# Weight stream of a graph and transformer kernel: one transfer for three weight blocks, on two semaphores, into the same six slots

## The chip, the cores and the metric

One Trainium2 chip, one core. The metric is the device time of one execution in microseconds (us); lower is better. Engines: TensorE (PE, its weight loads PEld), VectorE (DVE), ScalarE (ACT), GpSimd (POOL) and SyncE (SP), which here only issues the DMA transfers of the weight stream.

## The reference, cut to what matters

Four rounds over 512 nodes with 768 features. Each round adds a graph layer, an attention mixer and a feed-forward part to `x`. All work is matrix products in fp32 with 768x768 tiles of weights; the graph layers read 16,384 edges. The change touches only how weights reach the chip, so two of the feed-forward parts matter most. In round 1 (`ffn1` in the kernel) and in round 3 (`ffn3`), most weights meet few columns:

```
# round 1: 506 patch rows use fc1, fc2; 6 class rows use five small "atom" networks
patch_out = gelu(patch_tokens @ fc1_w.T + fc1_b) @ fc2_w.T + fc2_b
hid_all = gelu(einsum('bnd,ahd->bnah', cls_tokens, atom_in_w) + atom_in_b)
...
# round 3: 8 experts, each takes at most 64 of the 512 rows
expert_inputs = einsum('td,tec->ecd', xf, dispatch)
h = gelu(einsum('ecd,edm->ecm', expert_inputs, w1) + b1)
expert_outputs = gelu(einsum('ecm,emd->ecd', h, w2) + b2)
out = einsum('ecd,tec->td', expert_outputs, combine)
```

## The kernel before, in words

**The stream.** All weights but one lie in one DRAM tensor, `stream`, as blocks of 128 x 768 fp32 (384 KB), in the order of use. Six blocks are a turn; the kernel has 93 turns, 558 blocks (`TURNS`). On the chip `raw` has six slots, `raw[:, g, j]` with g = 0, 1 and j = 0, 1, 2; block b of each turn goes to slot g = b // 3, j = b % 3. SP (L317 to L338) issues one transfer per block, `load(n, b)`, on six semaphores `raw_in[b]`, one to a slot. It issues the first six at once. Each later one waits until that slot's previous block is free.

**Split stages.** In all parts but `ffn1` and `ffn3` each raw block is split by POOL in `split` (L354 to L363): `w_hi` is the block rounded to a shorter float, `w_lo` the rest. POOL waits for the load (`raw_in[b]`) and for TensorE to give back the split slot (`w_used`), then counts up `w_split`; with that the raw slot is free, and SP waits on `w_split` for the next load. TensorE makes three matmuls per tile from the split pairs (`mm3`, L409 to L416).

**Whole stages.** In `ffn1` (4 turns) and `ffn3` (6 turns), named in `WHOLE`, TensorE reads the raw slots itself. `whole_block(turn, b)` (L400) waits for `raw_in[b]`, and after a block `whole_block_used()` (L403, the matmul at L404) runs a tiny matmul that counts up `raw_used`, which SP waits for. `ffn1` multiplies at L971 (12 blocks; all but two meet 8 columns), then at L984 and L992 (12 blocks). `ffn3` has 16 blocks of 64 columns at L1056 and two that no one multiplies, and after ScalarE's last gelu (L1493) 18 blocks at L1069, in the last turn with 8 matmuls a block instead of 12. The tail behind them (L1077 and on) loads nothing.

**Stretches.** `stretches` lists runs of turns of one kind (split, whole, split, whole). At the start of each run SP waits on the semaphore of the run before, since those blocks hold the slots.

The matrix `L0_gnn_W1` is also loaded by ScalarE's own queue into a ring of eight slots (`w_ring`, `scr`), which the change does not touch.

Of the kernel before, what the change touches and what calls it, by code (L numbers as in the profile page):

```python
# [33 lines left out]
KC = D // P  # L34
# [149 lines left out]
def build(nc, t, out, only=None, LOOP_EVENTS={}):  # L184
# [3 lines left out]
    for p in parts:  # L188
        whole, n = p in WHOLE, sum(s[1] for s in stretches)
# [5 lines left out]
    with ctx:  # L195
        def sb(name, shape, dt=F32, where=ctx):
            return where.enter_context(nc.sbuf_tensor(name, shape, dt))

        def sem(name):
            return ctx.enter_context(nc.semaphore(name))  # L200

        raw = sb("raw", [P, 2, 3, KC, P])
# [91 lines left out]
        loaded, edges_in, rows_in, orf_in, sel_in = (sem(n) for n in ("loaded", "edges_in", "rows_in", "orf_in", "sel_in"))  # L295
        setup_done = sem("setup_done")
        pool_done = sem("pool_done")
        raw_in = [sem(f"raw_in{b}") for b in range(6)]
        w_high, w_split, w_used = sem("w_high"), sem("w_split"), sem("w_used")
        raw_used = sem("raw_used")  # L300
        tile_for = {"act": sem("tile_for_act"), "dve": sem("tile_for_dve")}
# [15 lines left out]

        @block.sync
        def _(sp):
            def load(n, b):  # L320
                sp.dma_start(raw[:, b // 3, b % 3], t["stream"][bass.ds(n * 6 + b, 1)].rearrange(
                    "o p (k c) -> (o p) k c", k=KC)).then_inc(raw_in[b], 16)

            for b in range(6):
                load(0, b)
            freed = raw_used if stretches[0][2] else w_split
            for n, (first, count, whole, before) in enumerate(stretches):
                if n > 0:

                    for b in range(6):  # L330
                        sp.wait_ge(freed, freed_turns * 6 + (b - 5))
                        load(first, b)
                freed, freed_turns = raw_used if whole else w_split, before + count
                with sp.Fori(1, count) as i:
                    for b in range(6):

                        sp.wait_ge(freed, i * 6 + (before * 6 + b - 5))
                        load(i + first, b)  # L338

        @block.gpsimd
        def _(pool):
            pool.memset(ident[:, :], 0.0).then_inc(pool_done, 1)
            pool.wait_ge(pool_done, 1)
            pool.affine_select(out=ident[:, :], in_=ident[:, :], compare_op=ALU.not_equal, fill=1.0, base=0,
                               pattern=[[-1, P]], channel_multiplier=1).then_inc(setup_done, 1)
            pool.iota(iota[:, :], pattern=[[1, N]], base=0, channel_multiplier=0).then_inc(setup_done, 1)
            pool.memset(ones[:, :], 1.0).then_inc(setup_done, 1)
            pool.memset(ones_r[:, :].bitcast(F32), 1.0).then_inc(setup_done, 1)
            pool.memset(ones_b[:, :], 1.0).then_inc(setup_done, 1)  # L350
            pool.memset(nv[:, :, :], 0.0).then_inc(setup_done, 1)
            pool.memset(hot[:, :, :, :], 0.0).then_inc(setup_done, 1)

            def split(turn, n, b):  # L354

                pool.wait_ge(raw_in[b], turn * 16 + 16)
                if n > 0:
                    pool.wait_ge(w_used, n * 6 + (b - 5))
                pool.tensor_scalar(w_hi[:, b // 3, b % 3], raw[:, b // 3, b % 3], 1.0, 1.0, ALU.mult, ALU.mult)\  # L359
                    .then_inc(w_high, 1)  # L360
                pool.wait_ge(w_high, n * 6 + (b + 1))
                pool.tensor_tensor(w_lo[:, b // 3, b % 3], raw[:, b // 3, b % 3], w_hi[:, b // 3, b % 3], ALU.subtract)\  # L362
                    .then_inc(w_split, 1)  # L363

            pool.wait_ge(setup_done, n_setup)
            for first, count, whole, before in stretches:
                if not whole:
                    for i in range(count):
                        for b in range(6):
                            split(first + i, before + i, b)  # L370
# [3 lines left out]
        def _(pe):  # L374
# [23 lines left out]
                          skip_group_check=True).then_inc(w_used, n)  # L398

            def whole_block(turn, b):  # L400
                pe.wait_ge(raw_in[b], turn * 16 + 16)

            def whole_block_used():  # L403
                pe.matmul(ps[0:2, 7, 0:2], ones_b[:, :], ones_b[:, :], start=True, stop=True,  # L404
# [2 lines left out]
            def first_turn(p):  # L407
                return sum(TURNS[q] for q in parts[:parts.index(p)])
# [544 lines left out]
            if part("ffn1"):  # L953
# [7 lines left out]
                turn = first_turn("ffn1")  # L961
                for n in range(2):
                    for f in range(KC):
                        q = 6 * n + f
                        c = slice(0, N if q < 2 else 8)
                        whole_block(turn + n, f)
                        use(f)
                        for k in range(KC):
                            if q == 0:
                                pe.wait_ge(dve_to_pe, normed[k])  # L970
                            mm = pe.matmul(ps[:, f, c], raw[:, f // 3, f % 3, k], acc[:, k, c], start=k == 0,  # L971
                                           stop=k == KC - 1, skip_group_check=True)
                        done(mm, f, "act")
                        whole_block_used()
                pe.wait_ge(dve_to_pe, S.due(dve_to_pe))
                for n in range(2):
                    for f in range(KC):
                        whole_block(turn + 2 + n, f)
                        if n == 0:
                            use(f)  # L980
                            for k in range(2):
                                if f == 0:
                                    pe.wait_ge(act_to_pe, S.due(act_to_pe))
                                mm = pe.matmul(ps[:, f], raw[:, f // 3, f % 3, k], scr[:, k], start=k == 0, stop=k == 1,  # L984
                                               skip_group_check=True)
                            done(mm, f, "dve")
                            if f == 0:
                                use(6)

                        o = ps[:, 6, (6 * n + f) * 8:(6 * n + f) * 8 + 8]  # L990
                        for k in range(2, KC) if n == 0 else range(KC):
                            mm = pe.matmul(o, raw[:, f // 3, f % 3, k], scr[:, 3, (6 * n + k) * 8 - 16:(6 * n + k) * 8 - 8],  # L992
                                           start=k == (2 if n == 0 else 0), stop=k == KC - 1, skip_group_check=True)
                        whole_block_used()
# [30 lines left out]
            if part("ffn3"):  # L1025
# [19 lines left out]
                turn = first_turn("ffn3")  # L1045
                for n in range(3):
                    for f in range(KC):
                        q = 6 * n + f
                        whole_block(turn + n, f)
                        if q < 16:  # L1050
                            use(f)
                            c = slice(64 * (q // 2), 64 * (q // 2) + 64)
                            for k in range(KC):
                                if q == 0:
                                    pe.wait_ge(act_to_pe, S.due(act_to_pe))
                                mm = pe.matmul(ps[:, f, c], raw[:, f // 3, f % 3, k], acc[:, k, c], start=k == 0,  # L1056
                                               stop=k == KC - 1, skip_group_check=True)
                            done(mm, f, "act")
                        whole_block_used()
                for n in range(3):  # L1060
                    if n == 0:
                        pe.wait_ge(act_to_pe, S.due(act_to_pe))
                    for f in range(KC):
                        whole_block(turn + 3 + n, f)
                        use(f)
                        for e in range(3 * n, min(3 * n + 3, 8)):
                            for h in range(2):
                                k, q = 2 * (e - 3 * n) + h, 2 * e + h
# [1410 lines left out]
```

## Time and profile before

| | before |
|---|---|
| median of 3 runs (lowest to highest) | 3600.44 us (3599.62 to 3601.2) |
| the profiled execution's own time | 3605.52 us |
| its span | 3603.7 us |
| TensorE busy | 3221.0 us (89%) |
| VectorE busy | 1747.3 us (48%) |
| GpSimd busy | 1420.6 us (39%) |
| ScalarE busy | 753.7 us (21%) |
| mean granted TensorE clock | 0.923 of 2.4 GHz |
| bytes moved by DMA | 256.76 MB, mean 71 GB/s |
| weight transfers | 558 of 384 KB |

### The profile page before, as it was taken

The page shows a single profiled execution, that of the slowest core. Times are in us where ns is not written, and L with a number is a line of the kernel's source. Part 1 is how long each engine was busy: PE and PEld are TensorE (multiplying, and loading weights), DVE is VectorE, ACT ScalarE, POOL GpSimd, SP SyncE. Part 2 cuts the span into 40 slices and gives each one's busy share as a digit, 9 for nine tenths or more (in the row PEclk, how much of TensorE's full clock was granted, in tenths as well). Part 3 has the DMA queues.
Part 4 walks back from the last instruction along what each step waited for, and adds up shares of the span by engine and source line. Part 5 has one row for each costly group of instructions (what it writes and reads, how often), then busy time and mean ns, then how long its engine had stood idle before and what let it go on. Part 6 is the DMA issues. An engine that isn't in the chain of part 4 may idle for free.

```text
span 3603.7 us, 41581 instructions
## 1 busy us (share of the span) xinstructions
PE 3221.0 (89%) x14631; PEld 2527.2 (70%) x14631; DVE 1747.3 (48%) x2950; ACT 753.7 (21%) x1318; POOL 1420.6 (39%) x1008
## 2 busy tenths in 40 slices
PE   8878988799999996998966698989999998979978
PEld 2356667678888884676755467768888886768868
DVE  6633359756554536336676514724333346651131
ACT  0133320033332312102123212211101112221122
POOL 2011137635344440563520013436676764426500
PEclk9989999799999996999978779989999999989977
DMA  2011136412122220232210041213232332213313
GB/s 75 5 35 31 31 107 219 152 49 75 57 61 73 74 69 13 68 92 62 74 40 9 1 132 49 66 55 94 90 96 89 103 93 73 64 41 92 92 36 115
DMA packets 91012, 256.76 MB, mean 71 GB/s; under 512 B 10287, under 2 KB 10927, under 8 KB 90612
## 3 DMA queue, kind: packets, MB, share of 16 engines
q1 hardware_dynamic: 80352, 219.45, 20.1%
q10 hardware_dynamic: 10548, 35.83, 2.8%
q8 instruction: 69, 1.13, 0.1%
q14 instruction: 43, 0.35, 0.0%
HBM read 253.67 MB, written 1.57 MB: 71 GB/s over the span
## 4 chain that ended last, share of the span: by engine, by line
PE 82%; DVE 10%; issue 4%; ACT 2%; POOL 1%; DMA 0%; DVEq 0%; ACTq 0%; POOLq 0%
PE ps L411 21%; PE ps L415 20%; PE ps L416 20%; PE ps L831 3%; PE ps L507 2%; PE ps L513 2%; PE ps L1069 1%; PE ps L743 1%; PE ps L940 1%; DVE aux L1695 1%; PE ps L736 1%; PE ps L722 1%; PE ps L971 1%; PE ps L726 1%; POOL w_lo L362 1%
## 5 line engine op out<-in xcount | busy, mean ns | idle before, releaser
L359 POOL TENSOR_SCALAR w_hi<-raw 128x768 fp32r<-128x768 f32 x498 | 454.4, 913 | 1949.1 <-PE ps L411 1579.0
L362 POOL TENSOR_TENSOR w_lo<-raw,w_hi 128x768 fp32r<-128x768 f32 x498 | 973.0, 1954 | 41.6
L411 PE MATMUL ps<-H_hi,w_hi 128*128 128x512 f32 x804 | 321.6, 400 | 36.0 <-issue 28.8
L411 PE MATMUL ps<-B_hi,w_hi 128*128 128x512 f32 x720 | 292.2, 406 | 32.7 <-DVE B_lo L1536 22.3
L415 PE MATMUL ps<-H_lo,w_hi 128*128 128x512 f32 x804 | 319.1, 397 | 0.0
L416 PE MATMUL ps<-H_hi,w_lo 128*128 128x512 f32 x804 | 318.5, 396 | 0.0
L411 PE MATMUL ps<-A_hi,w_hi 128*128 128x512 f32 x780 | 308.2, 395 | 0.0
L415 PE MATMUL ps<-A_lo,w_hi 128*128 128x512 f32 x780 | 304.9, 391 | 0.0
L416 PE MATMUL ps<-A_hi,w_lo 128*128 128x512 f32 x780 | 303.9, 390 | 0.0
L415 PE MATMUL ps<-B_lo,w_hi 128*128 128x512 f32 x720 | 284.5, 395 | 0.0
L416 PE MATMUL ps<-B_hi,w_lo 128*128 128x512 f32 x720 | 284.0, 394 | 0.0
L411 PEld LDWEIGHTS ps<-H_hi,w_hi 128*128 128x128 f32 x804 | 154.9, 193 | 76.4 <-issue 38.7
L1790 DVE TENSOR_TENSOR x<-ps,x 128x512 f32<-128x512 f32 x102 | 70.5, 691 | 273.6 <-PE ps L416 270.1
L411 PEld LDWEIGHTS ps<-B_hi,w_hi 128*128 128x128 f32 x720 | 137.5, 191 | 71.4 <-issue 42.2
L411 PEld LDWEIGHTS ps<-A_hi,w_hi 128*128 128x128 f32 x780 | 146.9, 188 | 44.6 <-issue 12.9
L416 PEld LDWEIGHTS ps<-H_hi,w_lo 128*128 128x128 f32 x804 | 154.8, 192 | 33.3
L415 PEld LDWEIGHTS ps<-H_lo,w_hi 128*128 128x128 f32 x804 | 154.8, 193 | 32.4 <-issue 0.2
L416 PEld LDWEIGHTS ps<-A_hi,w_lo 128*128 128x128 f32 x780 | 147.0, 188 | 31.2
L415 PEld LDWEIGHTS ps<-A_lo,w_hi 128*128 128x128 f32 x780 | 147.0, 189 | 29.2
L415 PEld LDWEIGHTS ps<-B_lo,w_hi 128*128 128x128 f32 x720 | 137.7, 191 | 30.2 <-issue 3.1
L416 PEld LDWEIGHTS ps<-B_hi,w_lo 128*128 128x128 f32 x720 | 137.5, 191 | 29.7
L411 PE MATMUL ps<-w_hi,H_hi 128*128 128x384 f32 x432 | 147.5, 342 | 3.0 <-ACT aux L1190 3.0
(423 smaller groups left out, 6206.5 us busy)
## 6 DMA issues: line engine op xcount, KB each, us to landing
raw<-stream_dram SPq DMA_DIRECT2D x558, 384.0 KB, 3.0
w_ring<-w_dram ACTq DMA_DIRECT2D x24, 384.0 KB, 3.6
scr<-w_dram ACTq DMA_DIRECT2D x24, 384.0 KB, 3.9
u_rows<-rows_dram ACTq DMA_DIRECT2D x8, 768.0 KB, 6.1
rows<-rows_dram ACTq DMA_DIRECT2D x7, 768.0 KB, 4.0
x<-x_dram ACTq DMA_DIRECT2D x1, 1536.0 KB, 8.9
out_dram<-x ACTq DMA_DIRECT2D x1, 1536.0 KB, 5.1
orf<-orf_dram ACTq DMA_DIRECT2D x3, 384.0 KB, 4.0
```

Of the source, the lines that this page charges most:

```text
L359: pool.tensor_scalar(w_hi[:, b // 3, b % 3], raw[:, b // 3, b % 3], 1.0, 1.0, ALU.mult, ALU.mult)\
L362: pool.tensor_tensor(w_lo[:, b // 3, b % 3], raw[:, b // 3, b % 3], w_hi[:, b // 3, b % 3], ALU.subtract)\
L411: mm = pe.matmul(o, wh, xh, start=first, stop=False, skip_group_check=True)
L415: pe.matmul(o, wh, xl, start=False, stop=False, skip_group_check=True)
L416: return pe.matmul(o, wl, xh, start=False, stop=last, skip_group_check=True)
L507: mm = pe.matmul(ps[:, 6], ones[:, :], norm_src[0][:, j], start=j == 0, stop=j == KC - 1, skip_group_check=True)
L513: mm = pe.matmul(ps[:, 7], ones[:, :], aux[:, j % 4], start=j == 0, stop=j == KC - 1, skip_group_check=True)
L722: done(pe.matmul(ps[:, 3 + m % 2, 0:ORF], k2[:, m * P:m * P + P], w, start=True, stop=True), 3 + m % 2, "act")
L726: done(pe.matmul(ps[:, 5 + r % 2], w[:, r * P:r * P + P], q2[:, :], start=True, stop=True), 5 + r % 2, "act")
L736: mm = pe.matmul(ps[:, 7, r * 68:r * 68 + 66], k_feat[:, m, r * P:r * P + P], vh[:, m, h], start=m == 0, stop=m == NT - 1, skip_group_chec ...
L831: mm = pe.matmul(ps[:, m], hot[:, c, 0, m * P:m * P + P], hot[:, c, 1, :], start=False, stop=False, skip_group_check=True)
L1790: ins = dve.tensor_tensor(dst[:, j], ps[:, j], dst[:, j], ALU.add)
```

## The change

One transfer now carries the three blocks of a half turn, `raw[:, g]`, and there are two semaphores instead of six. On the DRAM side the three blocks lie 384 KB apart, so the transfer reads, for each partition, three runs of 3 KB and writes them one behind the other. SP waits for the third of three freed blocks where it waited for each; the first value of that wait is that of `b` = 2 (or 5) before. POOL and TensorE wait on `raw_in[b // 3]` at each block, with the same value. The slots, their number and the order of the blocks stay.

```diff
--- before.py
+++ after.py
@@ -295,7 +295,7 @@
         loaded, edges_in, rows_in, orf_in, sel_in = (sem(n) for n in ("loaded", "edges_in", "rows_in", "orf_in", "sel_in"))
         setup_done = sem("setup_done")
         pool_done = sem("pool_done")
-        raw_in = [sem(f"raw_in{b}") for b in range(6)]
+        raw_in = [sem(f"raw_in{g}") for g in range(2)]
         w_high, w_split, w_used = sem("w_high"), sem("w_split"), sem("w_used")
         raw_used = sem("raw_used")
         tile_for = {"act": sem("tile_for_act"), "dve": sem("tile_for_dve")}
@@ -317,25 +317,25 @@
 
         @block.sync
         def _(sp):
-            def load(n, b):
-                sp.dma_start(raw[:, b // 3, b % 3], t["stream"][bass.ds(n * 6 + b, 1)].rearrange(
-                    "o p (k c) -> (o p) k c", k=KC)).then_inc(raw_in[b], 16)
-
-            for b in range(6):
-                load(0, b)
+            def load(n, g):
+                sp.dma_start(raw[:, g].rearrange("p j k c -> p j (k c)"), t["stream"][bass.ds(n * 6 + 3 * g, 3)].rearrange(
+                    "j p c -> p j c")).then_inc(raw_in[g], 16)
+
+            for g in range(2):
+                load(0, g)
             freed = raw_used if stretches[0][2] else w_split
             for n, (first, count, whole, before) in enumerate(stretches):
                 if n > 0:
 
-                    for b in range(6):
-                        sp.wait_ge(freed, freed_turns * 6 + (b - 5))
-                        load(first, b)
+                    for g in range(2):
+                        sp.wait_ge(freed, freed_turns * 6 + (3 * g - 3))
+                        load(first, g)
                 freed, freed_turns = raw_used if whole else w_split, before + count
                 with sp.Fori(1, count) as i:
-                    for b in range(6):
-
-                        sp.wait_ge(freed, i * 6 + (before * 6 + b - 5))
-                        load(i + first, b)
+                    for g in range(2):
+
+                        sp.wait_ge(freed, i * 6 + (before * 6 + 3 * g - 3))
+                        load(i + first, g)
 
 
         @block.gpsimd
@@ -353,7 +353,7 @@
 
             def split(turn, n, b):
 
-                pool.wait_ge(raw_in[b], turn * 16 + 16)
+                pool.wait_ge(raw_in[b // 3], turn * 16 + 16)
                 if n > 0:
                     pool.wait_ge(w_used, n * 6 + (b - 5))
                 pool.tensor_scalar(w_hi[:, b // 3, b % 3], raw[:, b // 3, b % 3], 1.0, 1.0, ALU.mult, ALU.mult)\
@@ -398,7 +398,7 @@
                           skip_group_check=True).then_inc(w_used, n)
 
             def whole_block(turn, b):
-                pe.wait_ge(raw_in[b], turn * 16 + 16)
+                pe.wait_ge(raw_in[b // 3], turn * 16 + 16)
 
             def whole_block_used():
                 pe.matmul(ps[0:2, 7, 0:2], ones_b[:, :], ones_b[:, :], start=True, stop=True,
```

SP's program at its start and in the loop of the first stretch (`ISA` is a semaphore wait, `REGISTER_ALU` works out a wait's value), as a difference, - before and + the change:

```order
 L318 UNCONDITIONAL_BRANCH
-L321 DMA raw<-stream_dram 128x768 x6
+L321 DMA raw<-stream_dram 128x3x768 x2
 L334 UNCONDITIONAL_BRANCH
 L334 ISA
 L321 ISA
-L321 DMA raw<-stream_dram 128x768
-L337 REGISTER_ALU
+L321 DMA raw<-stream_dram 128x3x768
 L321 ISA
```

Six issues of one block have become two of three, each behind one wait. On the other four engines every instruction stands in the place that it had.

## Rows read from the trace of the kernel before

**Rows 1.** The page: chain by engine; DMA issues with KB each, median us to landing

```profile
PE 82%; DVE 10%; issue 4%; ACT 2%; POOL 1%; DMA 0%; DVEq 0%; ACTq 0%; POOLq 0%
...
raw<-stream_dram SPq DMA_DIRECT2D x558, 384.0 KB, 3.0
...
rows<-rows_dram ACTq DMA_DIRECT2D x7, 768.0 KB, 4.0
x<-x_dram ACTq DMA_DIRECT2D x1, 1536.0 KB, 8.9
```

**Rows 2.** POOL's waits: engine, line, waited for; total us, times, longest us

```profile
POOL w_hi L359 <- PE ps L411: 1579.0, 177, 153.4
POOL w_hi L359 <- DMA raw<-stream_dram: 295.2, 2, 294.7
```

**Rows 3.** Timeline of POOL, six splits in a row: start us, duration us, instruction

```profile
2538.11 0.84 POOL L359 TENSOR_SCALAR w_hi<-raw 128x768 fp32r<-128x768 f32 x1 [9.17 <-PE ps L411]
...
2543.57 0.84 POOL L359 TENSOR_SCALAR w_hi<-raw 128x768 fp32r<-128x768 f32 x1
```

**Rows 4.** The tile raw in 2400 to 2900, 118 loads of 384 KB

```profile
DMA to landing us min/median/max: 2.7/3.0/3.3
```

**Rows 5.** Windows: stretch, length, busy us of each engine, granted clock, DMA share, GB/s

```profile
3499.72:3523.36 23.64, 23.64 (x196) 22.41 (x196) 0.00 (x0) 5.60 (x16) 0.00 (x0) 1.00 0.77 232
3524.13:3558.20 34.07, 34.07 (x156) 32.49 (x156) 0.00 (x0) 8.08 (x33) 0.00 (x0) 0.50 0.55 171
...
3528.00:3530.00 2.00, 2.00 (x11) 1.87 (x11) 0.00 (x0) 0.11 (x1) 0.00 (x0) 0.50 0.94 356
```

**Rows 6.** Timeline of PE, end of ffn1 and start of gnn2

```profile
2133.16 0.16 PE L404 MATMUL ps<-ones_b 128*2 128x2 bf16 x1
...
2166.33 0.66 PE L411 MATMUL ps<-w_hi,A_hi 128*128 128x384 f32 x1 [7.22 <-DVE A_lo L1539]
```

**Rows 7.** Timeline of ffn3, blocks 0 to 6: PE and SP's first reload

```profile
3499.72 0.16 PE L404 MATMUL ps<-ones_b 128*2 128x2 bf16 x1
...
3500.08 0.34 SPq L321 DMA_DIRECT2D raw<-stream_dram  x1
...
3502.87 0.16 PE L404 MATMUL ps<-ones_b 128*2 128x2 bf16 x1
...
3507.60 0.16 PE L404 MATMUL ps<-ones_b 128*2 128x2 bf16 x1
3507.70 1.55 PE L1056 MATMUL ps<-acc,raw 128*128 128x64 f32 x12
```

**Rows 8.** Timeline of PE in ffn1, blocks 2 to 6

```profile
2078.92 1.50 PE L971 MATMUL ps<-acc,raw 128*128 128x8 f32 x12
2080.36 0.16 PE L404 MATMUL ps<-ones_b 128*2 128x2 bf16 x1
...
2083.51 2.62 PE L971 MATMUL ps<-acc,raw 128*128 128x8 f32 x12
...
2086.15 2.73 PE L971 MATMUL ps<-acc,raw 128*128 128x8 f32 x12
```

**Rows 9.** DMA issues in 3500 to 3523: KB each, median us to landing

```profile
raw<-stream_dram SPq DMA_DIRECT2D x15, 384.0 KB, 3.8
```

**Rows 10.** Timeline of PE's weight loads, ffn3: block 15, gap, second half

```profile
3521.88 1.41 PEld L1056 LDWEIGHTS ps<-acc,raw 128*128 128x128 f32 x12
3523.36 0.11 PEld L404 LDWEIGHTS ps<-ones_b 128*2 128x2 bf16 x3
3524.13 2.63 PEld L1069 LDWEIGHTS ps<-exp,raw 128*128 128x128 f32 x12 [0.66 <-ACT junk L1099]
3526.88 0.08 PEld L404 LDWEIGHTS ps<-ones_b 128*2 128x2 bf16 x1
...
3529.72 0.08 PEld L404 LDWEIGHTS ps<-ones_b 128*2 128x2 bf16 x1
...
3558.28 1.78 PEld L1069 LDWEIGHTS ps<-exp,raw 128*128 128x128 f32 x8
```

## The prediction

> **What bounds the kernel now.** I read the page first, then who waits for loads, then the two stages that use the loaded blocks without a split. The profiled execution spans 3603.7 us and took 3605.52 us; the median of the runs shown is 3600.44, so 5.1 us are taken off the sum at the end. TensorE holds 82% of the chain that ended last, DMA 0% [rows 1]. So bytes bound nothing, and a change in how they are cut into transfers can only act by when a block is there. 558 transfers of 384 KB become 186 of 1152 KB; the bytes stay.
>
> Two kinds of reader exist. In the split stages POOL turns a raw block into high and low parts, and it waits almost always for TensorE to give back a split block: 1579.0 us in 177 waits. For a load it waited twice [rows 2]; one of the two, 294.7 us long, is only the stage in which it has no work. In ffn1 and ffn3 TensorE reads the raw slots itself, and there the ring of six slots is all the cover a load has. No row has TensorE waiting for a load today.
>
> **Split stages, costed at nothing.** The old load of block b went out when POOL had split block b. Now three go out when the third is split. POOL at full speed starts one split every 2.73 us and a new group of three after 8.2 us (5.46 us between its first and third start) [rows 3]; when TensorE paces it, it is slower still. So between the issue and the first split of those blocks lie three splits of the other group, 8.2 us. A single transfer lands after 3.0 us [rows 1, 4]. What one of 1152 KB needs is in no row of before. Bounds: 768 KB in one transfer took 4.0 us, 1.0 more than 384 KB, so a third 384 KB makes 5.0 [rows 1]; by the rate in a stretch with the queue nearly full (356 GB/s at a share of 0.94, 379 GB/s) the extra 0.786 MB cost 2.1 us, 5.1 in all; by the rate of the stage below (232 GB/s at 0.77, 301 GB/s) 2.6, 5.6 in all [rows 5]. The shortest single landing, 2.7 us [rows 4], gives 4.7 as the low end. The dearest row is x, 1536 KB in 8.9 us [rows 1], but it ran beside the first loads. I take 5.0, nearest to the 768 KB row, with 4.7 and 5.6 as ends. All lie under 8.2, so POOL never comes late. That would be the cover gone at a landing of 7.8 us.
>
> **SP, the start, and leaving ffn1, nothing.** SP issues 186 instead of 558 DMAs; it is on no path. At the start the edge lists, which the first matmuls wait for, share the DMA engines with the first six blocks; the bytes are the same in both kernels, and since the edge lists' own transfers go out with the first load in either, I bound this by half of one 1.0 us step of 384 KB [rows 1], 0.5 us either way. Behind ffn1, POOL's first group for gnn2 arrives when three last blocks are used and one landing is over: TensorE is done with the third block at 2133.2, so at 2133.2 + 0.36 + 5.0 = 2138.5 (the 0.36 is SP's, next part). It has split all six by 2138.5 + 6 x 2.73 = 2154.9, and TensorE first asks for them at 2166.3 [rows 6]. That cover is 11 us.
>
> **ffn1, nothing, though narrowly.** A block's last act is the small matmul L404; SP issues 0.36 us behind its start (3499.72 to 3500.08) [rows 7]. So a group comes back 0.36 + 5.0 = 5.36 us after its third block. In ffn1 the first group is done at 2080.36 and TensorE reaches the seventh block at 2086.15 [rows 8]: 5.8 us, a margin of 0.4; at 5.6 us of landing 0.2 us would be lost. From there twelve matmuls take 2.73 us and a group over 8.2, and nothing is late.
>
> **ffn3, first half (L1056): the term.** 16 blocks of 64-column matmuls at the full clock (granted 1.00, 2.4 GHz), one per 1.58 us (3502.87 to 3507.60 for three) [rows 5, 7]. Before, the slot of block b was refilled behind block b, with five blocks (7.9 us) of cover for 3.8 us [rows 9]. Now slots 0 to 2 are refilled behind block 2: issue 3503.23, landed 3508.23. TensorE wants block 6 at 3507.70, 0.1 behind L404. 0.53, with the wake-up **a pause of 0.55 us** in a stage that had none.
>
> What the pause does to the clock is worth more than the pause. Behind block 15 there is such a gap already: TensorE's weight loads stood idle 0.66 us waiting for ScalarE's gelu. Before the gap twelve weight loads took 1.41 us, behind it 2.63, the granted clock was 0.50 (1.2 GHz), and it stayed there for the next 34 us of the same 64-column work [rows 5, 10]. In ffn1 the same fall came without a gap, within 5 us of the first 8-column block (twelve matmuls 1.50 us at 2078.92, 2.62 at 2083.51 [rows 8]). So this work holds the full clock only just and does not win it back. I take it that the clock falls some 2 us behind the first pause. Of blocks 6 to 15, 1.3 then run at 1.58 us and 8.7 at 2.84 (L404 at 3526.88 and 3529.72 [rows 10]): 8.7 x 1.27 = **11.0 us**. At 2.84 us a block a group takes 8.5 us and covers 5.36, so no second pause follows.
>
> The Trainium skill, page "TensorE: Matmul & The Clock Gate", section "Why this matters for your kernels", warns only of idle gaps much longer than these. By it the 0.55 us would leave the clock up. The trace disagrees in the one place that shows such a gap, and I go by the trace; the page's rule is rival A.
>
> **ffn3, hand-over and second half (L1069).** Its first group is refilled behind block 14. TensorE gets there after block 15 (2.84 us) and the gelu (0.77 us, 3523.36 to 3524.13 [rows 10]), 3.61 us; the group takes 5.36: **1.75 us**. Then groups take 8.5 us, and 6.0 in the last turn (three blocks of 8 matmuls, weight loads 1.78 us, some 2 us a block [rows 10]), both over 5.36: nothing more. The clock is at 1.2 GHz there in both kernels.
>
> **Sum.** 0.55 + 11.0 + 1.75 = 13.3 us. 3605.5 + 13.3 = 3618.8 for the profiled execution, 3600.4 + 13.3 = **3613.7 us** for the median, slower by 0.37%. With a landing of 4.7 it is 12.7 (if so short a pause, 0.25 us, still drops the clock), with 5.6 it is 14.5.
>
> **The rivals.** About 0.2%, 7.2 us, is what a measurement of this kernel can tell from no change.
>
> A, not slower beyond that: the pause comes, but the clock stays at 2.4 GHz through blocks 6 to 15. The point that decides is whether 0.55 us idle is enough; 0.66 us was. Then the first half pays 0.55 us for group 2 and 0.5 for group 4 (released behind group 2, two groups on), and the hand-over 5.36 - 1.58 - 0.77 = 3.0 us: 4.1 us in all, 3604.5. Chance 0.20. For it speaks that the gap seen before stood beside an idle wait for another engine and behind three small matmuls, not inside the run of blocks.
>
> B: the clock holds over the first pause and falls after the second, at 3518. Then 2.7 blocks less run at full clock, 3.4 us, and with 1.05 of pauses and 1.75 of hand-over it is 6.2 us, 3606.6. Chance 0.07.
>
> C: three blocks land within 4.47 us (the point at which 3507.70 is met). No pause in the first half, the clock stays, only the hand-over remains: at 4.4 us 0.36 + 4.4 - 2.35 = 2.4 us, 3602.8. The minimum of 2.7 us for one speaks for it, the 768 KB row against. Chance 0.05.
>
> D: larger transfers bring the bytes sooner and something gains. It would have to be TensorE or POOL waiting for loads, and neither does [rows 1, 2]. So no gain, 3600.4, and a faster kernel only by 1 or 2 us of luck at the start. Chance 0.03. The Trainium skill, page "DMA: Bandwidth & Descriptors", section "Bandwidth", says to batch transfers to 1 MiB or more for most of the peak rate. That is a rule for kernels that wait for bytes, and by it this rival is all the change can be.
>
> E: interleaving three strips makes a transfer as slow as x, 8.9 us, 9.3 with the issue. Then every group of ffn3 and ffn1 is late. 4.4 us at the first pause, 12.7 of clock, 5.6 at the hand-over, 3.3 in the last turn, some 6 in the other groups: 32 us, 3632. Chance 0.03.
>
> **The numbers.** The forecast has 0.62. Slower by over 0.2% are the forecast and E, 0.65. Within 0.2% are A, B, C and 0.01 of D, 0.33. Faster is what is left of D, 0.02. The range reaches from C and A below (3602.5) past the forecast at a landing of 5.6 us (3614.9) with 2 us for where the clock falls (3617). It leaves out E and D and the ends of the forecast.
>
> **What would show it.** In the changed profile: raw transfers of 1152 KB landing in 5.0 us; a row with TensorE waiting for raw at L1056, 0.3 to 1.2 us, near 3508; the granted clock at 0.50 from about 3510 instead of 3524; the L1056 weight loads with a mean near 270 ns; a wait of 1 to 3 us for raw at the first L1069. Everything up to 3498 should stand where it stood, within 1 us. The forecast is wrong if the L1056 blocks keep 1.58 us to the end (A or C), and its premise is wrong if POOL shows new waits for raw in a split stage or the span differs before 3498.

## The result, and the profile after

The change makes the kernel slower by 0.55%, more than forecast.

| | before | after |
|---|---|---|
| median of 5 runs, taken side by side | 3600.44 us (3599.18 to 3603.66) | 3621.55 us (3616.6 to 3622.5) |
| after / before, with its 95% interval | | 1.0055 [1.004, 1.0069] |
| the profiled execution's own time | 3605.52 us | 3622.5 us |
| its span | 3603.7 us | 3620.7 us |
| mean granted TensorE clock | 0.923 | 0.919 |

The medians stand 21.1 us apart, the two profiled executions 17.0. Single executions of the kernel before, over all its runs in this study, took from 3595.9 to 3607.4 us, so a pair of profiles can be some microseconds off the medians either way. The profiled execution of before was 5.1 us above its median, that of the change 1 us; so this pair shows too small a difference, and the last part says where.

The page of the changed kernel: the chain by engine, then the weight transfers (count, KB each, median us from issue to landing), which answer to [rows 1].

```profile
PE 81%; DVE 10%; issue 4%; ACT 2%; POOL 1%; DMA 1%; DVEq 0%; ACTq 0%; SPq 0%; POOLq 0%
...
raw<-stream_dram SPq DMA_DIRECT2D x186, 1152.0 KB, 5.4
```

DMA is now 1% of the chain, so somebody does wait for loads. The waits by engine and line (us in total, times, longest us) say who.

```profile
POOL w_hi L359 <- PE ps L411: 1572.0, 177, 152.7
POOL w_hi L359 <- DMA raw<-stream_dram: 303.9, 3, 300.2
...
PE ps L971 <- DMA raw<-stream_dram: 1.4, 1, 1.4
PE ps L992 <- DMA raw<-stream_dram: 1.0, 1, 1.0
PE ps L1056 <- DMA raw<-stream_dram: 0.9, 1, 0.9
```

POOL is nearly as before [rows 2], with three waits for loads instead of two. Apart from the stage without work (300.2 us, 294.7 before), it waited 0.5 us for loads before and 3.7 now: 2.5 at its first split, and 1.25 for the second group behind ffn1. TensorE had no wait for a load; now it has three, 3.3 us in all. That is about a sixth of the loss. Most of the rest is what happens behind them. Timeline of TensorE's weight loads in ffn3 (start us, duration us; in brackets the idle time before it and what ended it), then SP's:

```profile
3503.94 0.08 PEld L404 LDWEIGHTS ps<-ones_b 128*2 128x2 bf16 x1
...
3508.66 0.08 PEld L404 LDWEIGHTS ps<-ones_b 128*2 128x2 bf16 x1
3509.72 1.41 PEld L1056 LDWEIGHTS ps<-acc,raw 128*128 128x128 f32 x12 [0.97 <-DMA raw<-stream_dram]
...
3511.29 2.43 PEld L1056 LDWEIGHTS ps<-acc,raw 128*128 128x128 f32 x12
...
3513.93 2.63 PEld L1056 LDWEIGHTS ps<-acc,raw 128*128 128x128 f32 x12
...
3539.54 2.63 PEld L1069 LDWEIGHTS ps<-exp,raw 128*128 128x128 f32 x12 [2.82 <-issue]
```

```profile
3504.30 0.38 SPq L321 DMA_DIRECT2D raw<-stream_dram  x1
```

Read it in this order. Block 2 ends with its small matmul at 3503.94, and SP issues the transfer for slots 0 to 2 at 3504.30. It lands 5.4 us later, at 3509.7. Block 5 ended at 3508.66, so block 6 starts 0.97 us late. It still runs at full speed (1.41 us for twelve weight loads), the next takes 2.43, and all behind it 2.63. That is the clock, which the windows show (length, busy us by engine, granted clock, DMA share, GB/s), to be read against [rows 5]:

```profile
3500.78:3508.66 7.88, 7.88 (x66) 7.47 (x65) 0.00 (x0) 2.46 (x6) 0.00 (x0) 1.00 0.43 133
3511.29:3536.61 25.32, 25.32 (x117) 24.14 (x116) 0.00 (x0) 2.83 (x9) 0.00 (x0) 0.51 0.41 142
3539.54:3573.00 33.46, 33.42 (x153) 31.99 (x154) 0.00 (x0) 8.08 (x33) 0.00 (x0) 0.50 0.39 135
```

In the kernel before the granted clock was 1.00 up to 3523.36. Here it is 0.51 from 3511.29 on, and TensorE is busy all the time, so nothing else slows these blocks. The groups of 3498 to 3590 (count, busy us, mean ns; idle before) give the stage in one row for each kernel, first the change, then the kernel before:

```profile
L1056 PEld LDWEIGHTS ps<-acc,raw 128*128 128x128 f32 x192 | 33.5, 267 | 1.3 <-DMA raw<-stream_dram 1.0
```

```profile
L1056 PEld LDWEIGHTS ps<-acc,raw 128*128 128x128 f32 x192 | 22.8, 191 | 0.3
```

**Where the 17.0 us of the two profiles lie**, by the same instruction in both:

| piece | us later |
|---|---|
| at 3473, ahead of ffn3 | +1.1 |
| first half of ffn3: pause | +1.0 |
| first half of ffn3: slower clock | +11.2 |
| hand-over (block 15's L404 3523.36 and 3536.61, first L1069 3524.13 and 3539.54) | +2.2 |
| behind the first L1069, to the end | +1.6 |

The kernel is already late 20 us after its start. Timelines of POOL's first split, VectorE's first operation and the end of POOL's sixth split, first before, then after:

```profile
4.64 0.83 POOL L359 TENSOR_SCALAR w_hi<-raw 128x768 fp32r<-128x768 f32 x1 [0.49 <-DMA raw<-stream_dram]
...
5.76 1.68 DVE L1970 CAST src_f<-src_i 128x128 f32<-128x128 int32 x1 [5.76 <-DMA dst_i<-dst_dram]
...
19.13 1.80 POOL L362 TENSOR_TENSOR w_lo<-raw,w_hi 128x768 fp32r<-128x768 f32 x1
```

```profile
6.66 0.83 POOL L359 TENSOR_SCALAR w_hi<-raw 128x768 fp32r<-128x768 f32 x1 [2.52 <-DMA raw<-stream_dram]
7.54 0.23 DVE L1970 CAST src_f<-src_i 128x128 f32<-128x128 int32 x1 [7.54 <-DMA dst_i<-dst_dram]
...
21.19 1.80 POOL L362 TENSOR_TENSOR w_lo<-raw,w_hi 128x768 fp32r<-128x768 f32 x1
```

Two things come later. The first split starts when three blocks are there instead of one, 2.0 us later, and the sixth ends 2.1 us later. And VectorE starts 1.8 us later: it waits for the second edge list (`dst_i`, 64 KB on ScalarE's queue), which landed 6.3 us after its issue and 4.5 us in the kernel before. No engine waits for these splits yet. But VectorE, which builds the one-hot matrices of the edges, is slow beside them. Its operation on the changed kernel's timeline, beside a split and behind the last:

```profile
13.02 1.97 DVE L1976 TENSOR_SCALAR hot<-iota,dst_f 128x512 bf16<-128x512 int16 x1
...
25.49 0.35 DVE L1976 TENSOR_SCALAR hot<-iota,dst_f 128x512 bf16<-128x512 int16 x1
```

Such an operation takes 0.91 or 1.97 us while POOL splits and 0.35 behind it, and TensorE waits 0.83 us for each pair. In the kernel before it runs at 0.34 from 21.00 us on, here from 23.06 us. TensorE is free of that wait from 21.40 us before and from 23.20 after, 1.8 us later. The Trainium skill says in "GPSIMD Engine Reference", section "Specifications", that GpSimd shares its SBUF interfaces with VectorE, and that VectorE instructions in a two-port mode or with two SBUF inputs contend for them. This trace agrees that there is contention, with these durations; whether the operation here is of one of these kinds no run shows.

### The profile page after: what moved, and what is told of

The parts are those of the page before. It is cut to its first block, busy times and chain, and to the rows that moved or that the text cites. A ratio compares the mean times of both kernels' runs of the same rounds, so it can differ in the third digit from the quotient of the medians.

```text
span 3620.7 us, 40141 instructions
## 1 busy us (share of the span) xinstructions
PE 3228.8 (89%) x14631; PEld 2534.6 (70%) x14631; DVE 1746.9 (48%) x2950; ACT 753.8 (21%) x1318; POOL 1419.1 (39%) x1008
## 4 chain that ended last, share of the span: by engine, by line
PE 81%; DVE 10%; issue 4%; ACT 2%; POOL 1%; DMA 1%; DVEq 0%; ACTq 0%; SPq 0%; POOLq 0%
PE ps L411 21%; PE ps L415 20%; PE ps L416 20%; PE ps L831 3%; PE ps L507 2%; PE ps L513 1%; PE ps L1069 1%; PE ps L743 1%; PE ps L940 1%; DVE aux L1695 1%; PE ps L736 1%; PE ps L722 1%; PE ps L726 1%; PE ps L1056 1%; PE ps L971 1%
## 5 line engine op out<-in xcount | busy, mean ns | idle before, releaser
L415 PEld LDWEIGHTS ps<-B_lo,w_hi 128*128 128x128 f32 x720 | 137.7, 191 | 30.0 <-issue 3.1
```

Of the source, the lines that this page charges most:

```text
L415: pe.matmul(o, wh, xl, start=False, stop=False, skip_group_check=True)
```

## The experiments

Line numbers shift by a few lines where an edit stands above them: L1058, L1060, L1062 and L1065 are L1056 of the kernel before, and L1071, L1074, L1076 and L1078 are L1069. Ratios are to the kernel before, measured side by side on the same chip, with the 95% interval. Several kernels have the transfer size by stretch. `load(n, b, s)` moves `s` blocks in one transfer and counts up the semaphore of the first, and `sizes` holds `s` for the stretches up to ffn1, ffn1, up to ffn3, and ffn3. The core of that edit to the kernel before, the same in all of them:

```diff
-            def load(n, b):
-                sp.dma_start(raw[:, b // 3, b % 3], ...).then_inc(raw_in[b], 16)
+            def load(n, b, s):
+                sp.dma_start(slots.rearrange(...), t["stream"][bass.ds(n * 6 + b, s)]...).then_inc(raw_in[b], 16)
...
-                    for b in range(6):
-                        sp.wait_ge(freed, i * 6 + (before * 6 + b - 5))
+                    for b in range(0, 6, s):
+                        sp.wait_ge(freed, i * 6 + (before * 6 + b + s - 1 - 5))
```

**Does a pause alone make the clock fall?** The kernel before, with single transfers. Block 6 of ffn3 also waits for the load of block 9, which lands about as late as a triple would.

```diff
                         whole_block(turn + n, f)
+                        if q == 6:
+                            whole_block(turn + 1, 3)
```

> The kernel before with one wait more: at the seventh block of ffn3 (L1056) TensorE also waits for the load of the tenth, which lands some 0.9 us after TensorE would have begun. Every load and transfer stays as before. Theory (the pause drops the clock): TensorE idles 0.9 us there, the granted clock falls to 0.50 within some 2 us, eight to nine blocks of L1056 take 2.84 us instead of 1.58, so +0.9 + 8.6 x 1.27 = +12 us, 3612, and no pause at the hand-over. Rival (the clock falls for another reason, such as large transfers beside the matmuls): only the pause, +0.9 us, 3601.

3614.24 us (3613.14 to 3617.56) against 3602.7 (21 runs), ratio 1.0036 [1.0023, 1.0048]. Weight loads, then a window:

```profile
3502.57 0.08 PEld L404 LDWEIGHTS ps<-ones_b 128*2 128x2 bf16 x1
3503.36 1.42 PEld L1058 LDWEIGHTS ps<-acc,raw 128*128 128x128 f32 x12 [0.71 <-issue]
...
3504.94 2.21 PEld L1058 LDWEIGHTS ps<-acc,raw 128*128 128x128 f32 x12
...
3507.36 2.63 PEld L1058 LDWEIGHTS ps<-acc,raw 128*128 128x128 f32 x12
```

```profile
3505.00:3530.00 25.00, 25.00 (x117) 23.85 (x116) 0.00 (x0) 2.82 (x9) 0.00 (x0) 0.51 0.51 149
```

One pause of 0.71 us, the only edit, and the clock is down for the rest of the stage: 11.5 us. Nothing of the change is in this kernel but the pause. This carries most of the loss.

**The change in ffn3 alone**, `sizes = [1, 1, 1, 3]`.

> Only the last stretch of turns (ffn3) is loaded by transfers of three blocks; all else by single ones. Theory (the loss sits in ffn3): nearly the whole of the +21 us, 13 to 20 us, 3614 to 3620; pause near 1 us at the seventh block, clock at 0.50 from there. Rival (part of the loss comes from the start and the split stages, of which the trace of the change shows 1.1 us at 3473 but the medians differ by more): under +13 us here and the rest in the run with single loads in the whole stages.

3615.68 us (3614.02 to 3620.48), ratio 1.0042 [1.0025, 1.0059], 13.0 us more. The pause and the hand-over:

```profile
3501.42 1.42 PEld L1065 LDWEIGHTS ps<-acc,raw 128*128 128x128 f32 x12 [0.85 <-DMA raw<-stream_dram]
...
3531.06 2.64 PEld L1078 LDWEIGHTS ps<-exp,raw 128*128 128x128 f32 x12 [2.73 <-issue]
```

ffn3 alone gives 13 of the 21 us, about the sum forecast for the whole change. What is left, 5 to 8 us, must come from the other stretches, as far as it is more than spread (4 runs here).

**Is it the later issue, or that three blocks land as one?** Single transfers on six semaphores, but in ffn3 all three of a group go out behind the third block.

```diff
-                        sp.wait_ge(freed, i * 6 + (before * 6 + b - 5))
+                        sp.wait_ge(freed, i * 6 + (before * 6 + b - 5 + (2 - b % 3 if n == 3 else 0)))
```

(The wait at the start of a stretch has the same term.)

> The kernel before, single transfers on six semaphores, but in ffn3 SP issues them three at a time, when the third slot of a group is free, as the change does. It tells the late issue from the one semaphore for three blocks. Theory A (it is the landing of all three that TensorE waits for): the first block of a group lands some 3.5 us after its issue, before TensorE wants it, so no pause in the first half, the clock stays up to the last block, and at the hand-over 0.36 + 3.5 - 2.35 = 1.5 us: +1.5 us, 3602. Theory B (the late issue itself makes the pause): a pause at the seventh block, the clock falls, +13 us or more.

3603.47 us (3601.44 to 3608.53), ratio 1.0003 [0.9993, 1.0012]. Window, and the hand-over:

```profile
3495.00:3517.00 22.00, 22.00 (x184) 20.85 (x183) 0.00 (x0) 5.04 (x16) 0.00 (x0) 1.00 0.62 215
```

```profile
3520.03 2.63 PEld L1069 LDWEIGHTS ps<-exp,raw 128*128 128x128 f32 x12 [1.76 <-issue]
```

No pause and the full clock through the first half; only the hand-over is 1.1 us longer. So the later issue alone is nearly free. The first block of a group has its own semaphore here and is there ahead of the other two, while in the change it counts as there when all three are.

**Pairs in all stretches**, `sizes = [2, 2, 2, 2]`.

> Transfers of two blocks (768 KB) everywhere, three semaphores. A pair lands some 4.2 us after its issue, 4.6 us behind its second block. In L1056 two pairs of 3.15 us = 6.3 us cover that: no pause in the first half; at the hand-over the pair was freed behind the fourteenth block, TensorE wants it after two blocks and the gelu, 3.9 us: 0.7 us. Theory (what counts is landing against the cover of the remaining slots, not the size as such): +0.7 us and +1 us at the start as in the run with the split stages alone, 3603 to 3605. Rival (any larger transfer lowers the clock): +12 us.

3604.29 us (3600.39 to 3608.13), ratio 1.0005 [0.9995, 1.0014].

```profile
raw<-stream_dram SPq DMA_DIRECT2D x279, 768.0 KB, 4.3
```

```profile
3521.82 2.42 PEld L1078 LDWEIGHTS ps<-exp,raw 128*128 128x128 f32 x11 [1.42 <-ACT junk L1108]
```

A pair lands in 4.3 us and has four blocks, 6.3 us, of cover: no pause in the first half, and 0.8 us at the hand-over (1.42 instead of 0.66). Six slots stand pairs and don't stand triples.

**Triples in the split stretches alone**, `sizes = [3, 1, 3, 1]`, measured twice.

> The change in the split stages only; ffn1 and ffn3 are loaded by single transfers again. Theory: no pause in ffn3, L1056 blocks 1.58 us to the end, and only the 1.1 us that the changed kernel is late at 3473: +1 us, 3600 to 3603. Rival (the split stages pay): +5 us or more. POOL waits for no load but at the start and behind ffn1 in both.

> Transfers of three blocks in the split stages alone, again. Theory: +1 to +3 us, from POOL's first six splits, which end 2 us later and slow VectorE in the edge stage that long. Rival (they cost nothing that can be measured): 0.

3603.74 us (3600.96 to 3607.68), ratio 1.0004 [0.9994, 1.0013]; the second time 3606.13 (3601.41 to 3609.78) against 3601.88, ratio 1.0013 [1.0003, 1.0022]. Its first split starts 2.0 us late, as in the change. The two intervals overlap, and only the second leaves out 1: the medians say a small loss, 1.0 and 4.3 us.

**Triples in the whole stages alone**, `sizes = [1, 3, 1, 3]`, and **in ffn1 alone**, `sizes = [1, 3, 1, 1]`.

> Transfers of three blocks in ffn1 and ffn3, single ones in the split stages: the half of the change that the run with the split stages alone leaves out. Theory (the parts add, the rest is spread between executions): +15 us, 3616 to 3618, and the change beside it 1 to 3 us above this. Rival (split and whole stages together cost 4 us or more that neither costs alone): 3615 here and 3621 for the change on the same chip.

> Transfers of three blocks in ffn1 alone. The profile of the change has a pause of 1.44 us for a load at the seventh block of ffn1, another execution of it 0.7 us. Theory (a small loss of its own, the clock is at 0.50 there in any case): +0.5 to +1.5 us, 3603. Rival (ffn1 holds the 6 us that lie between the 13 us of ffn3 alone and the 20 us of the change): +5 us.

The first: 3617.23 us (3614.01 to 3621.8) against 3601.88, ratio 1.0043 [1.003, 1.0057], 15.4 us more. The second: 3601.19 us (3597.11 to 3604.55) against 3601.26, ratio 0.9998 [0.9989, 1.0008]. ffn1 has a pause in it (0.65 us in the profile), and no loss that can be measured.

**The change again**, twice.

> The changed kernel again, to measure its distance to the kernel before on one chip with more runs: the run with ffn3 alone gave +13.0 us and the one with the split stages alone +1.0, while the first measurement of the change gave +21. Theory (the loss sits in ffn3 and the two parts add up): +14 us, 3617, with the rest of the 21 being spread from run to run. Rival (the two parts together cost more than each, in ffn1 or behind it): +18 us or more again.

> The changed kernel on the same chip as the two halves of it. Theory: the sum of the two halves within 2 us, some +16 to +19 us. Rival: 4 us or more above their sum.

3622.27 us (3618.37 to 3626.42), ratio 1.0055 [1.0041, 1.0069]; 3620.42 us (3619.97 to 3622.9), ratio 1.0053 [1.0039, 1.0067]. Its loss is 20.3 us against 3601.93 and 18.5 against 3601.88. The parts alone give 15.4 and 1.0 to 4.3, 16.4 to 19.7 in sum: they add up within what a median is uncertain.

**Is the start the split stretches' loss?** In the changed kernel SP lets the edge lists land before its first load.

```diff
+            sp.wait_ge(edges_in, 32)
             for g in range(2):
                 load(0, g)
```

> The changed kernel, but SP issues the first weight loads only when both edge lists have landed. In the profile of the change VectorE begins at 7.54 us (5.76 before), and the kernel stays 1.5 us late to TensorE's row at 40 us. Theory (the larger first transfers hold the edge lists back): VectorE begins at 5 us or sooner, the edge stage 2 to 3 us sooner than in the change, the rest alike: 3622 - 2.5 = 3619. Rival (the late start has another cause): VectorE at 7.5 us as in the change, no difference.

3619.12 us (3616.9 to 3621.9), ratio 1.0044 [1.0029, 1.006]: 17.9 us more than the kernel before, where the change itself was 18.5 to 21.1 us more. VectorE's timeline, and the window of 15 to 30 us:

```profile
4.25 0.23 DVE L1971 CAST src_f<-src_i 128x128 f32<-128x128 int32 x1 [4.25 <-POOL hot L353]
...
6.34 0.35 DVE L1977 TENSOR_SCALAR hot<-iota,src_f 128x512 bf16<-128x512 int16 x1
...
17.56 1.97 DVE L1977 TENSOR_SCALAR hot<-iota,dst_f 128x512 bf16<-128x512 int16 x1
```

```profile
15.00:30.00 15.00, 8.76 (x21) 2.04 (x20) 15.00 (x11) 0.00 (x0) 14.58 (x11) 0.64 0.25 87
```

VectorE starts at 4.25 us instead of 7.54 and runs at 0.35 us an operation until POOL's splits begin. But these now start at 13.80 us instead of 6.66 and last until 30.3, the operations beside them take 0.91 and 1.97 again, and TensorE's granted clock is 0.64 there on average (1.00 in the kernel before and in the change). VectorE's last one-hot operation starts at 138.15 us, in the change at 138.05. No gain that can be measured. The edit moves both late things at once, VectorE's start forward and the splits back, so it does not tell what each costs; how the start's loss is to be had back stays open.

**Was the gap at the hand-over what dropped the clock in the kernel before?** The same reason, used the other way. Two matmuls of 512 columns on data that is there, into a PSUM bank nobody reads at that point, keep TensorE busy while it waits for the last gelu. They are the only edit.

```diff
+            def filler(n):
+                for _ in range(n):
+                    pe.matmul(ps[:, 7], ones[:, :], acc[:, 0], start=True, stop=True, skip_group_check=True)
...
                     if n == 0:
+                        filler(2)
                         pe.wait_ge(act_to_pe, S.due(act_to_pe))
```

> The kernel before with two matmuls more (512 columns, fp32, into the unused bank 7) where TensorE waits for the last gelu of ffn3, between L1056 and L1069. They fill the 0.66 us gap and cost some 0.2 us behind it. Theory (the idle gap drops the clock): the clock stays at 1.00 through L1069, 12 blocks at 1.58 instead of 2.85 us and 6 at 1.1 instead of 1.99: 15.2 + 5.3 = 20 us faster, 3582. Rival (the clock would fall in L1069 anyway): +0.2 us.

3581.76 us (3579.28 to 3585.61), ratio 0.9943 [0.993, 0.9957]: 20.2 us **faster** than the kernel before. A window of the second half, and its weight loads in one row:

```profile
3523.50:3549.50 26.00, 26.00 (x212) 24.23 (x210) 0.00 (x0) 11.41 (x46) 0.00 (x0) 1.00 0.72 229
```

```profile
L1074 PEld LDWEIGHTS ps<-exp,raw 128*128 128x128 f32 x192 | 22.9, 191 | 0.7 <-issue 0.5
```

The row of the kernel before for the same work, for comparison:

```profile
L1069 PEld LDWEIGHTS ps<-exp,raw 128*128 128x128 f32 x192 | 42.3, 329 | 0.9 <-ACT junk L1099 0.7
```

19.4 us less weight-load time for the same 192 rows. With the gap filled the clock stays at 1.00 through all 18 blocks. So the 0.66 us of idle time had cost 20 us all along, and the 64-column work can hold the full clock, as long as nothing interrupts it.

**Can the change be mended the same way?** The changed kernel with three fillers ahead of blocks 6 and 12 and seven at the hand-over.

```diff
+                        if q in (6, 12):
+                            filler(3)
                         whole_block(turn + n, f)
...
                     if n == 0:
+                        filler(7)
```

> The changed kernel with matmuls of the same kind where TensorE waits for a load: 3 (1.3 us) ahead of the seventh and the thirteenth block of ffn3, 7 (3.0 us) at the hand-over. The landings stay late. Theory: the fillers stand in for idle time, the clock stays at 1.00, so the pauses cost their own length, 1.3 x 2 + 3.0 = 5 us at most, and L1069 gains the 20 us: 3602 - 15 = 3588. Then a pause at every second group of L1069 may come (a group of 4.7 us against a landing of 5.4): if one drops the clock, half of the gain goes, 3595 to 3600. Rival (pauses as such cost, the clock follows the transfers): 3620 as the change.

3609.71 us (3604.93 to 3611.56), ratio 1.0021 [1.0011, 1.003]: 12.6 us better than the change beside it (3622.27) and 7.8 above the kernel before, short of both figures. Two windows, the place between them, and the fillers:

```profile
3500.00:3528.00 28.00, 28.00 (x203) 23.96 (x202) 0.00 (x0) 5.54 (x16) 0.00 (x0) 1.00 0.52 170
3546.00:3570.00 24.00, 24.00 (x111) 22.79 (x110) 0.00 (x0) 6.00 (x24) 0.00 (x0) 0.50 0.42 146
```

```profile
3545.14 2.63 PEld L1076 LDWEIGHTS ps<-exp,raw 128*128 128x128 f32 x12 [0.81 <-DMA raw<-stream_dram]
```

```profile
L409 PE MATMUL ps<-acc,ones 128*128 128x512 f32 x26 | 12.0, 604 | 0.0
```

The first half keeps the full clock. At full clock a triple is late again in the second half (0.81 us at 3545.14), and there the clock falls. And the fillers were twice as long as I had reckoned: an fp32 matmul shows as two entries, so 13 fillers are 26 entries and 12.0 us. Enough cover is cheaper than filling the holes.

**The two best edits together**, on the kernel before: two fillers, and the edge lists first.

> The kernel before with the two filler matmuls behind L1056 (-20 us when tried) and with the first weight loads behind the edge lists. Theory: both gains add, 20 us and some 1 us (VectorE begins at 5 us instead of 5.76), 3580 to 3581. Rival (the late weights hold something else up, x and the small tables load beside them): 3582 or more, and VectorE no sooner.

3580.56 us (3578.43 to 3586.84), ratio 0.9943 [0.993, 0.9957]. That cannot be told from the fillers alone. Its last one-hot operation even starts later than with the fillers alone, at 138.05 us instead of 135.95. The kernel to keep is the one before with two fillers.

## Why the prediction was right or wrong

The main mechanism was right and in the place named, the size too small: 13.3 us forecast, 21.1 in the medians (18.5 and 20.3 when repeated), and the time lies above the range. The step that failed is a term put at nothing, the start with the split stages; the landing was also taken a little too short.

**The landing, 5.0 us taken, 5.4 measured** in ffn3, within the bounds of 4.7 to 5.6. It enters twice: the pause was 0.97 us (0.55 forecast), the hand-over cost 2.2 us (1.75). The 768 KB row that I leaned on (4.0 us) belonged to another queue; the same size on SP's queue took 4.3 (pairs). The rate of the neighbouring stage, which gave 5.6, was as near. This term is 0.9 us short.

**The clock, 11.0 us forecast, 11.2 measured.** Full speed held for the one block behind the pause, as assumed, and the fall came within the next. The pause-only kernel shows the cause by itself. **Rival A falls** with it: 0.71 us of idle time was enough, as 0.66 us had been. The Trainium skill's page "TensorE: Matmul & The Clock Gate", section "Why this matters for your kernels", warns only of idle gaps much longer; in this kernel's 64-column fp32 blocks the measurements disagree with it in three places (0.66, 0.71 and 0.97 us). That the clock is not won back in this work held in every kernel (25 us here, 34 us before). That the work holds it "only just" did not: with the hand-over filled, ffn3 keeps 1.00 through both halves, and what brings it down is the gap. For ffn1 this is not shown; there the weight loads slow down to 2.33 us from 2084.42 on, ahead of its first pause, and no run tried to stop that. B falls as well, since there was no second pause, and C, since the landing was over 4.47.

**Split stages and start, costed at nothing: the step that failed, 1 to 4 us.** The steady part was right: POOL never came late within a stage. So was leaving ffn1: its first group came at 2138.1 (2138.5 forecast), long before TensorE asks for it. What failed is the start, bounded at 0.5 us because the bytes are the same. With the same bytes, the first block is there only with the third, so the splits start 2.0 us later; and the edge list, issued at the same time as before, lands 1.8 us later. Both move the stretch in which the splits slow VectorE, on which TensorE waits. What each of them costs no run separates. I had asked who waits for the splits and not what runs beside them. By the prediction's own sign, new waits of POOL for loads in a split stage, its premise was wrong here.

The one pair of profiles makes this look small: 1.8 us lost by 23 us, 1.1 left at 3473. The other profiles show that it is more, when the start of the same instruction is read in each (us):

| instruction | the kernel before | six others with single first loads | six with triples there, the change among them | mean difference |
|---|---|---|---|---|
| VectorE's first | 5.76 | 5.65 to 6.15 | 7.35 to 7.75 | 1.7 |
| last of VectorE's 256 one-hot operations | 136.4 | 135.4 to 136.2 | 137.7 to 139.3 | 2.5 |
| TensorE's first matmul of ffn3 | 3498.3 | 3491.2 to 3497.2 | 3496.4 to 3500.6 | 4.1 |

(The mean difference is that of the six with triples from all seven others. The six others are the runs of the pause, of ffn3, of ffn1 and of the whole stages alone, of the late issue and of the two fillers. The six with triples are the change, its two repeats, the two measurements of the split stretches alone and the change with fillers.) The start costs 2.5 us, and there the two groups lie apart. Further on they overlap, and whether more is lost than these 2.5 us stays open. The profiled execution of the kernel before was the latest of its seven at the last two places, 3.2 us above their mean at the first matmul of ffn3, though nothing differs between these programs up to there but the loads of ffn1 in two of them. That is where the 17.0 us of the one pair fall short of the 18.5 to 21.1 of the medians. The two measurements of the split stretches alone, 1.0 and 4.3 us, lie on both sides of 2.5.

**ffn1, costed at nothing, "narrowly": wrong in the trace, not in the time.** The first pause is there:

```profile
2088.30 2.64 PEld L971 LDWEIGHTS ps<-acc,raw 128*128 128x128 f32 x12 [1.44 <-DMA raw<-stream_dram]
```

That one transfer took 6.6 us to land, above my upper end, against 5.8 us of cover. The wait was 0.54 and 1.14 us in the change's repeats, 1.48 with the whole stages and 0.65 with ffn1 alone changed. And there is a second one that the prediction ruled out:

```profile
2133.69 2.64 PEld L992 LDWEIGHTS ps<-scr,raw 128*128 128x128 f32 x12 [1.13 <-DMA raw<-stream_dram]
```

It said that from block 6 on twelve matmuls take 2.73 us. But the granted clock comes back to 1.00 late in ffn1, and three L992 blocks ahead of this wait took 1.4 us each, too little cover for a group. That the time does not show these 2.6 us is luck: from the first L971 to the first wide matmul behind ffn1 (2166.33 in the kernel before) both kernels took 100.2 us, since the granted clock from 2115.6 to 2132.5 was 1.00 in the change and 0.87 before. In the repeats this way took 100.4 and 103.1 us, in kernels with single loads in ffn1 about 97.2 or 100.2. So ffn1's share of the loss is not known better than its own run says: nothing, between 4 us less and 3 us more.

**The hand-over: right in kind**, 2.2 us. **Behind it I had nothing, and 1.6 us were lost in this profile**: the granted clock goes up, down and up there in the tail. But from the last L1069 to the end the profiles take 33.5 or 35.1 us (32.6 with the two fillers), and both are seen with the change: 35.1 here and in its first repeat, 33.5 in its second. 35.1 was also seen with the late issue, the pairs and the pause, 33.5 in the kernel before and with the split stretches alone. What decides it stays open, so this is no sure part of the loss.

**The sum.** Of the 7.8 us missing, 0.9 is the landing, 0.2 the clock, 2.5 the start (up to 4 with the split stretches), and 0 or 1.6 the tail, together 3.6 to 6.7. Of the change's repeats, with 18.5 and 20.3 us of loss, 5.2 and 7.0 were missing. What is left, 1 to 4 us in the first measurement, is within the spread of medians. The range was wrong for the same reason. It held the ends of ffn3's terms, and nothing for terms at zero that turn out small and positive, nor for the spread of single executions, 12 us for this kernel.

**D falls**: there is no gain anywhere, as nothing waited for bytes. The rule of the Trainium skill that I weighed there (page "DMA: Bandwidth & Descriptors", section "Bandwidth": batch to 1 MiB or more) costs time here: 1152 KB transfers lose 18.5 to 21.1 us, 768 KB ones nothing that can be measured. What the kernel needs is the first block early, not the bytes at a high rate. **E falls** by the landing, 5.4 us and not 8.9.

## What to carry to other kernels

Before batching loads into a ring, compare issue-to-landing of the batch with the cover that is left when the batch's last slot comes free (here three blocks, 4.7 us, against 0.36 + 5.4), stage by stage, and mind that the first block of a batch now counts as there with its last. Price a short idle time of TensorE by what the granted clock does behind it, not by its length; where the clock falls at such a gap and stays down in dense work, try a matmul or two in the gap (two did it here). And when an edit delays work that nobody waits for, look at what runs beside it.

## What the runs showed of the hardware that was not expected

- Idle times of 0.66, 0.71 and 0.97 us each took TensorE's granted clock from 1.00 to 0.50 in fp32 matmuls of 64 columns, and 25 to 34 us of unbroken work of that kind did not bring it back. Two matmuls of 512 columns in the gap kept it at 1.00 for 26 us, worth 20.2 us.
- One transfer of 384, 768 and 1152 KB landed after 3.0, 4.3 and 5.4 us (medians of their kernels): a little over 1 us for each further 384 KB.
- A VectorE operation of 0.35 us took 0.91 or 1.97 us beside GpSimd's fp32 splits.
- Letting the small transfers go first started VectorE 3.3 us earlier and gained nothing measurable, with the splits, and the slow stretch beside them, 7.1 us later.
- A list of 64 KB, issued at the same time (1.2 us), landed after 6.3 us beside two first transfers of 1152 KB and after 4.5 us beside single ones of 384 KB.
